# Perceiver layer on one core: the last key's share of attention moves from a matmul to a VectorE multiply-add

## The reference

```python
x = x + xattn(layernorm(x), ctx)      # softmax(q k^T / 16) v over 257 keys, one head of 256, (x + attended) @ Wo.T + bo
x = x + mixer(layernorm(x))           # in-proj to 512, 3-tap conv, silu, delta, scan over 32 steps with 16 states, out-proj
x = x + ffn(layernorm(x))             # gated, hidden 1024, inputs and weights rounded to few levels
```

## Time and profile before

| | before |
|---|---|
| median of 3 runs | 1037.6 us (1036.54 to 1038.55) |
| the profiled execution, its own time | 1038.41 us |
| its span, first to last instruction | 1036.3 us |
| busy: PE, DVE, POOL, ACT | 90%, 86%, 82%, 73% of the span |
| mean granted TensorE clock | 0.979 |

### The profile page before, as it was taken

The page is one execution under the profiler, slowest core; times in us unless marked ns, Lnnn a source line. Parts: engine busy times, 40 slices in busy tenths (PEclk is TensorE's granted clock), DMA queues, the critical chain, the costliest instruction groups (busy, mean ns, idle before and its releaser), DMA issues.

```text
span 1036.3 us, 13057 instructions
## 1 busy us (share of the span) xinstructions
PE 935.2 (90%) x4158; PEld 507.5 (49%) x4192; DVE 894.7 (86%) x1216; ACT 756.8 (73%) x1322; POOL 852.3 (82%) x616
## 2 busy tenths in 40 slices
PE   8986988999899998999899998999899998768897
PEld 6643453546345454546345554546345554434464
DVE  1636888899989999899989999899989999899964
ACT  2256658877897859877897859877897869765655
POOL 1069998899979898899979898899979898899920
PEclk9998989999999999999999999999999999988999
DMA  9814710344042610544042610544042300500000
GB/s 353 336 36 172 291 41 11 153 164 183 0 171 96 224 42 2 183 164 183 1 171 88 232 41 2 183 161 186 1 152 109 128 0 2 183 0 0 1 21 21
DMA packets 21915, 116.33 MB, mean 112 GB/s; under 512 B 3479, under 2 KB 4119, under 8 KB 9304
## 3 DMA queue, kind: packets, MB, share of 16 engines
q1 hardware_dynamic: 16232, 80.70, 21.0%
q10 hardware_dynamic: 5616, 34.81, 9.3%
HBM read 111.04 MB, written 4.46 MB: 111 GB/s over the span
## 4 chain that ended last, share of the span: by engine, by line
PE 26%; DVE 24%; ACT 19%; POOL 17%; issue 12%; DMA 1%; ACTq 0%; DVEq 0%; POOLq 0%
DVE state L1158 14%; POOL state L849 11%; PE acc L1312 11%; PE bank L1312 10%; ACT decay L920 6%; PE decay L1312 3%; POOL state L857 3%; DVE raw L1136 2%; ACT u L1019 2%; ACT u L1027 2%; ACT L920 2%; ACT soft L904 2%; DVE hm L1236 1%; POOL rstd L810 1%; DVE sg L1221 1%
## 5 line engine op out<-in xcount | busy, mean ns | idle before, releaser
L1158 DVE TENSOR_TENSOR_SCAN state<-decay,state 128x512 f32<-128x512 f32 (+1 forms) x352 | 590.7, 1696 | 35.1 <-ACT decay L920 22.8
L849 POOL TENSOR_TENSOR state<-w,brep 128x512 f32<-128x512 f32 (+1 forms) x352 | 612.0, 1766 | 0.5 <-POOL w L882 0.5
L1312 PE MATMUL acc<-state,ident 128*128 128x512 f32 x832 | 410.1, 610 | 13.7 <-DVE state L1158 12.3
L920 ACT ACTIVATE decay<-delta,neg_a 128x496 f32<-128x496 f32 x512 | 329.5, 669 | 88.1 <-DVE state L1158 86.7
L1312 PEld LDWEIGHTS acc<-state,ident 128*128 128x128 f32 x832 | 149.8, 193 | 160.5 <-issue 117.6
L857 POOL TENSOR_TENSOR state<-state 128x512 f32<-128x512 f32 x96 | 121.9, 1270 | 48.5 <-DVE state L1158 47.6
L1312 PE MATMUL bank<-out_w,u 128*128 128x256 f32 x256 | 58.2, 383 | 8.7 <-DVE u L1145 8.7
L1312 PE MATMUL bank<-xn_t,in_w 128*128 128x512 f32 x128 | 60.3, 604 | 5.0 <-DVE u L1304 3.4
L904 ACT ACTIVATE soft<-x_in,nmr,rstd 128x256 f32<-128x256 f32 x64 | 33.2, 589 | 43.0 <-POOL nmr L813 43.0
L952 ACT ACTIVATE sg<-bank,ag 128x512 f32<-128x512 f32 x64 | 43.6, 681 | 25.6 <-PE bank L1312 24.8
L1312 PEld LDWEIGHTS bank<-out_w,u 128*128 128x128 f32 x256 | 47.8, 190 | 22.8 <-DVE u L1145 15.8
(11 more groups left out here) (171 smaller groups left out, 1345.5 us busy)
## 6 DMA issues: line engine op xcount, KB each, us to landing
keys<-in_keys_t SPq DMA_DIRECT2D x32, 1028.0 KB, 5.8
brep<-b_scratch ACTq DMA_DIRECT2D x32, 1024.0 KB, 7.3
keys<-in_keys_n SPq DMA_DIRECT2D x29, 1024.0 KB
out<-x_in SPq DMA_DIRECT2D x16, 256.0 KB, 5.9
x_in<-in_x SPq DMA_DIRECT2D x14, 256.0 KB
u<-in_keys_n SPq DMA_DIRECT2D x1, 1024.0 KB
w<-in_keys_n SPq DMA_DIRECT2D x1, 1024.0 KB
delta<-in_keys_n SPq DMA_DIRECT2D x1, 1024.0 KB
```

The costliest lines, as they stand in the source:

```text
L849: nc.gpsimd.tensor_tensor(state[g % CPT][:, 0:count * tok].rearrange("p (c t) -> p c t", c=count), w[:, m, 0:tok].unsqueeze(1).to_broadcas ...
L920: last = nc.scalar.activation(decay[:, q:q + groups * GSEQ, 1:LEN], d, ACT.Exp, scale=neg_a[:, m, n + i:n + i + 1])
L1158: nc.vector.tensor_tensor_scan(flat, by, flat, 0.0, ALU.mult, ALU.add).then_inc(scan_done, 1)
L1312: return nc.tensor.matmul(o, l, r, start=first, stop=last)
```

## The change

1. `p_last`, the third transpose of `p_turn`, the `pl_t` copy of `p_evac`, and the 128x256 matmul of `attend` go, and so do `own_seq` (a 2 KB load), `pl_t` and four POOL memsets at the start.
2. The load of `keys_l` now spreads each of the four rows over 32 partitions: 128 rows, 128 KB a group. SP issues it once `z_ready` of the group two before has come, not `z_done`.
3. A new part `p_norm` on ACT multiplies the 257 weights by `rsum` before they are turned; it waits for DVE's `p_sum`.
4. `z_evac` moves from ACT to DVE: one multiply-add, z = `keys_l` x weight 256 + the PSUM sum. It waits for the matmuls of `attend` and for the keys' load.
5. All tables of "pre" and the "post" tables of phases 2 to 7 are written anew. The tables of phases 8 and 9 and the preparation are the same.

```diff
-                    if b == 0 and g < 2:
-                        sp.wait_ge(prep_p, PREP_P)
-                    else:
-                        reach(sp, z_done, *((b, g - 1) if g >= 2 else (b - 1, GROUPS - 1 + g)))
-                    sp.dma_start(keys_l[g % 2][0:GSEQ, :], t["keys_l"][FIRST_GROUP[b] + g]).then_inc(loaded, 16)
+                    if b or g >= 2:
+                        reach(sp, z_ready, *((b, g - 1) if g >= 2 else (b - 1, GROUPS - 1 + g)))
+                    sp.dma_start(keys_l[g % 2][:, :], t["keys_l"][FIRST_GROUP[b] + g].unsqueeze(1)
+                                 .to_broadcast((GSEQ, LEN, DIM))).then_inc(loaded, 16)
...
                     elif part == "exp":
                         after(act, p_turned, b, g - 1)
+                        after(act, z_ready, b, g - 1)
...
-                    elif part == "p_last":
-                        reach(act, probs_ready, b, g + 1)
-                        after(act, p_turned, b, g)
-                        nc.scalar.activation(p_last[:, :], own_seq[:, :], ACT.Copy,
-                                             scale=probs[g % 2][:, KEYS - 1:KEYS]).then_inc(p_last_ready, 1)
+                    elif part == "p_norm":
+                        reach(act, rsum_ready, b, g + 1)
+                        nc.scalar.activation(probs[g % 2][:, :], probs[g % 2][:, :], ACT.Copy, scale=rsum[:, g:g + 1])\
+                            .then_inc(p_normed, 1)
...
-                        nc.scalar.activation(to_l[0:GSEQ, :], bank[0:GSEQ, of, 2 * P:3 * P], ACT.Copy)\
-                            .then_inc(p_t_ready, 1)
-                    elif part == "z_evac":
-                        reach(act, z_done, b, g + 1)
-                        reach(act, rsum_ready, b, g + 1)
-                        after(act, z_turned, b, g if scan else g - 1)
-                        nc.scalar.activation(att_buffers(g, scan)[2][:, :], bank[:, att_banks(g, scan)[1], 0:DIM], ACT.Identity, scale=rsum[:, g:g + 1])\
-                            .then_inc(z_ready, 1)
...
+                    elif part == "z_evac":
+                        reach(dve, z_done, b, g + 1)
+                        if b == 0:
+                            dve.wait_ge(first_n_loaded[g], 32)
+                        else:
+                            reach(dve, keys_n_loaded[g % 2], b - 1, 32 * (g // 2 + 1))
+                        after(dve, z_turned, b, g if scan else g - 1)
+                        nc.vector.scalar_tensor_tensor(att_buffers(g, scan)[1][:, :], keys_l[g % 2][:, :],
+                                                       probs[g % 2][:, KEYS - 1:KEYS],
+                                                       bank[:, att_banks(g, scan)[1], 0:DIM], ALU.mult, ALU.add)\
+                            .then_inc(z_ready, 1)
...
-                        nc.tensor.transpose(bank[0:GSEQ, to, 2 * P:3 * P], p_last[:, :], ident[:, :]).then_inc(p_turned, 1)
...
-                        mm(bank[:, att_banks(g, scan)[1], 0:DIM], att_buffers(g, scan)[1][:, :], keys_l[g % 2][:, :], True, False)
```

More of the change, by code:

```diff
@@ L110 @@
[L110 to L114, removed]
+    ("z_evac", [30, 34, 63, 63]),
+    ("b_load", [78, 78, 78, 85]),
+    ("p_turn", [19, 25, 42, 42]),
+    ("s_neg", [4, 12, 25, 33]),
+    ("stats1", [0]),
+    ("x_proj", [85]),
+    ("attn_out", [65, 67]),
+    ("q_evac", [7]),
+    ("x_dbl", [76]),
+    ("evac2", [73]),
+    ("attend", [22, 33, 43, 47]),
+    ("stats2", [72]),
+    ("rstd1", [5]),
@@ new lines @@
+    ("softplus", [77, 81]),
+    ("s_bias", [4, 17, 28, 33]),
+    ("query", [1]),
+    ("add2", [40]),
+    ("dt", [87, 87, 87, 87]),
+    ("zt_evac", [23, 38, 71, 72]),
+    ("turn1", [0]),
+    ("evac1", [5]),
+    ("u_evac", [74, 74, 75, 75]),
+    ("xn2", [72]),
+    ("mix_in", [72, 73, 75, 84]),
+    ("rstd2", [21]),
+    ("exp", [7, 17, 21, 43]),
+    ("p_evac", [13, 30, 68, 70]),
+    ("add1", [7]),
+    ("p_norm", [12, 19, 42, 44]),
+    ("s_max", [1, 1, 22, 24]),
+    ("score", [4, 4, 14, 24]),
@@ L144 @@
[L144 to L157, removed]
+    ("exp", [15, 22, 28, 34]),
+    ("query", [10]),
+    ("attend", [16, 29, 30, 40]),
@@ new lines @@
+    ("p_norm", [15, 24, 31, 34]),
+    ("p_evac", [15, 28, 32, 38]),
+    ("x1", [52, 54]),
+    ("s_neg", [15, 22, 26, 32]),
+    ("q_evac", [11]),
+    ("rstd2", [51]),
+    ("s_bias", [16, 22, 26, 32]),
+    ("p_sum", [16, 23, 27, 33]),
+    ("rstd1", [0]),
+    ("add1", [45]),
+    ("stats2", [54]),
+    ("turn1", [3]),
+    ("add2", [64]),
+    ("evac1", [8]),
+    ("tap2", [61, 64, 69, 70]),
+    ("evac2", [58]),
+    ("x_proj", [73]),
+    ("softplus", [79, 87]),
+    ("z_evac", [20, 29, 32, 44]),
@@ L158 @@
+    ("silu", [69, 70, 70, 70]),
 ]
 PRE = [
-    ("x_dbl", [72]),
[L161 to L176, removed]
@@ L195 @@
[L195 to L199, removed]
+    ("xn1", [5]),
+    ("turn2", [55]),
+    ("softplus", [83, 87]),
+    ("exp", [13, 23, 29, 39]),
+    ("attn_out", [46, 46]),
+    ("score", [5, 10, 23, 28]),
+    ("xn2", [53]),
+    ("s_neg", [14, 17, 27, 34]),
+    ("rstd1", [0]),
+    ("x1", [51, 52]),
+    ("s_bias", [14, 18, 28, 38]),
+    ("mix_in", [57, 57, 59, 61]),
+    ("stats2", [52]),
@@ L200 @@
+    ("z_evac", [24, 28, 38, 43]),
+    ("tap2", [60, 61, 66, 66]),
+    ("evac1", [7]),
+    ("u_evac", [58, 60, 62, 64]),
+    ("p_norm", [17, 25, 30, 41]),
+    ("q_evac", [9]),
+    ("p_evac", [20, 25, 32, 42]),
+    ("b_load", [80, 82, 84, 84]),
+    ("p_sum", [16, 24, 29, 39]),
 ]
 PRE_END = [
-    ("x_dbl", [72]),
[L203 to L209, removed]
@@ new lines @@
+    ("zt_evac", [25, 31, 39, 45]),
+    ("z_turn", [24, 28, 39, 44]),
+    ("s_max", [13, 16, 25, 31]),
+    ("evac2", [55]),
+    ("tap0", [60, 61, 63, 65]),
+    ("x_proj", [67]),
+    ("attend", [20, 26, 32, 43]),
+    ("add2", [66]),
+    ("z_evac", [24, 28, 38, 43]),
+    ("tap2", [60, 61, 66, 66]),
+    ("evac1", [7]),
+    ("u_evac", [58, 60, 62, 64]),
+    ("p_norm", [17, 25, 30, 41]),
+    ("q_evac", [9]),
+    ("p_evac", [20, 25, 32, 42]),
+    ("b_load", [80, 82, 84, 84]),
+    ("p_sum", [16, 24, 29, 39]),
@@ L291 @@
+    ("h_scale", [22, 32, 59, 74]),
+    ("h_turn", [25, 34, 68, 76]),
+    ("h_evac", [30, 35, 71, 80]),
+    ("x_turn", [7]),
+    ("h_max", [19, 28, 54, 69]),
+    ("hidden", [15, 18, 22, 26, 42, 48, 63, 68]),
+    ("stats3", [5]),
+    ("scale_x", [12]),
 ]
```

272 lines of the change are left out of this document (109 added, 163 removed).

## The result

The changed kernel is slower: 1046.83 us median of 7 runs (1045.4 to 1052.38) against 1040.55 us of the kernel before beside it (7 runs, 1036.54 to 1043.32), a ratio of 1.0074 with a 95% interval of 1.0054 to 1.0095. The profiled execution has a span of 1045.2 us; before it was 1036.3 us. The difference of 8.9 us between these two executions (the ratio says 5.6 to 9.9 us over many) lies in two places and is reduced in two others, read from the starts of the first `w` on POOL and of each block's last `y` on DVE: +4.96 us ahead of the scan (the first `w` starts at 81.17 instead of 76.21), -0.5 in phase 1, +6.5 over phases 2 to 7, -2.1 in phase 8.

A forecast was written before the change was run, and what follows sets the result against it. The six steady phases decide, DVE and PE nearly tied: 1.56 - 0.65 - 0.71 - 0.3 = -0.1 us a phase, -0.6 in all, start and phase 1 zero, giving 1037.0 us; own range 1035.5 to 1039.7, 8-in-10 range 1029 to 1046.

The forecast's parts named there:

- rival 1: Steady phases: the gaps to be filled hang on DVE itself and move along; +0.9 us a phase, 1043 us; chance 0.32.
- Order, steady phases: Phases 2 to 7: new places fill DVE's idle gaps against 1.56 us of added work; -0.1 us a phase.
- (a): Steady phase: x_max goes from step 9 to 12, so one more scan fills DVE's 0.65 us gap; -0.65 us.
- (b): Steady phase: DVE's 0.71 us wait for PE at the second y goes; -0.71 us.
- Start: Phase 0: 0.7 us for larger keys_l loads and 0.8 for two z_evac, against PE's relief before x1; zero.
- rival 3: Start: the four-row source confines the load to 4 of 16 engines; +1.8 us, 1038.8; chance half of 0.37.
- VectorE's added work: Steady phase: four z_evac on DVE at 0.39 us each (bound 0.47), 1.56 us a phase.
- The wait for attend 3: Fourth z_evac on DVE: attend 3 ends at 715.8, DVE arrives at about 717; no wait, loss if PE over 1.2 late.
- TensorE's relief: PE's gapless stretch, 701 to 719 us: 1.1 us of work goes, only 0.71 us can reach the end.
- Rival 2: Steady phases: TensorE was the bound, its 1.1 us of relief comes out in full; -6.6 us, 1031; chance 0.31.
- (c): End of a phase: finish 2 one slot earlier spares ACT a 0.45 us wait, 0.3 counted; finish 3 gains nothing.
- (d): Steady phase: add1 on POOL moves to a time when POOL is ahead of DVE; nothing, given 11.6 us of slack.

The follow-up runs named there:

- e13: e1 with each DVE z_evac done twice from the second phase on, the first into a tile nobody reads; ratio 1.0157, phase 119.04 us.
- e4: Kernel before without the third transpose, its copy and the keys_l matmul, order unchanged; 1034.59 us, ratio 0.9971, phase 116.37 us.
- e10: e1 with x_max put back from step 12 to its old step 9; ratio 1.0056, phase 117.48 us.
- e1: Changed kernel with the last keys laid out 32 times each, so the load's source has 128 rows, not four; ratio 1.0066, phase 117.47 us.
- e6: Kernel before with z_evac as a multiply by rsum on DVE, PE's last-key work kept; 1056.64 us, ratio 1.0187, phase 118.40 us.
- e14: e1 with a 128x256 matmul of last-key rows ahead of each attend again, result overwritten, from the second phase on; 1054.01 us, ratio 1.0148, phase 118.69 us.
- e11: Kernel before with only the third finish and last h_turn at their new steps and down 2 at step 74; ratio 0.9996, phase 116.46 us.
- e8: Kernel before with the changed kernel's two feed-forward tables and nothing else; ratio 1.0150, phase 118.60 us.
- e5: e1 with z_evac as a plain copy on ACT, without the last key's share; 1056.6 us, ratio 1.0177, phase 118.23 us.
- e3: Kernel before with only the keys_l load made the 128 KB broadcast from four rows; ratio 1.0064, first w at 82.86 us.
- e2: Changed kernel with the old 4 KB keys_l load, the last key's share added for four rows only; ratio 1.0041, first w at 76.83 us.
- e9: e1 with z_evac on 32 of the 256 columns from the second phase on; ratio 1.0033, phase 117.03 us.

## Why the prediction was wrong

Forecast were 1037.0 us, no change, with the mechanism of rival 1 at 0.32 and 1043. Measured was a ratio of 1.0074, which is 1045.3 us on the 1037.6 of the forecast: above its own range, at the slow end of the wide one. Two steps failed.

- **Order, steady phases, (a) and (b): the gaps of 0.65 and 0.71 us take 1.36 of the 1.56 us.** This is the step that failed. Both gaps closed and two others of 0.88 and 0.70 us opened, one for ACT's `tanh`, one for PE's `attend`; so the idle time stayed. The phase grew by 1.01 us where -0.1 was forecast. For the wait at the fourth `z_evac` it is shown that it is a delay between two of DVE's own instructions and moves along with them: in e13 the eviction comes 1.17 us later and its wait is 0.70 us as before. e4 shows it for the second `y` (PE relieved, the wait of 0.71 us still 0.62, its chain starting from a scan). For the gap of 0.65 us there is only e10, where it changes places with the 0.88 us at no gain. It is rival 1, which had +0.9 us a phase, with the signs that the prediction gave for it: a phase over 117.4 us and over 6 us of DVE idle.
- **Start: zero, or +1.8 us by the four-row source.** Measured is +4.96 us. The mechanism of rival 3 is shown by e1 in the queue: with the same bytes from 128 rows the next issue takes 0.64 instead of 5.51 us, and the scan starts 3.34 us sooner (2.8 to 3.5 in the four profiles with a like clock). The Trainium skill ("DMA: Bandwidth & Descriptors", Rules for kernel authors) has the rule that an outermost dimension of size c below 16 confines a DMA to at most c engines. By that rule a source of four rows is slower, and e1 agrees; how many engines carried it no row here shows. The term was too small: I counted 64 KB more on four engines, 2.6 us of transfer instead of 0.7, and let 1.8 us of that reach `x1`. The queue behind the load was late by 3.6 us, and the second add of `x1` starts at 55.86 us, 3.7 later than before. The other 1.2 us lie behind that add, where the forecast had nothing, at a granted clock of 0.93 instead of 1.00. I had said that such a delay would show at the first abs sum, at 39 us; it came at 41.52, held up by a `z_evac`.
- **VectorE's added work, 0.39 us each.** Right: 0.40 us from start to start, and 0.39 in e13, where all of it came out.
- **The wait for attend 3, priced at nothing.** Wrong: 0.70 us. I let DVE reach it at about 717 and PE at 715.8, as if the two were independent. Placed by the distance from the last `y`, DVE reaches it at 716.9, as forecast, and PE is done at 717.6, 1.8 us later than forecast; 1.2 was the bound that I gave for a loss. Sums stand ahead of `attend` that wait for a scan, and the eviction starts 4.2 us behind that scan even where PE had been idle for 0.57 us (e13). Nor does PE's relief get there: in e4 `attend` 3 starts 0.4 us earlier, not 1.1. In the old order with the eviction on DVE (e6) the phase grows by 1.92 us, 0.36 more than four paces.
- **TensorE's relief: at most 0.71 us of 1.1 to show.** By itself it shows nothing (0.11, e4). In the new order it shows 1.22 (e14). The relief was also over-sized: PE's busy time fell to 108.0 us a phase, not to the 107 expected. Rival 2 therefore had a real mechanism, but it pays for part of the change instead of making it a gain: without it the phase would be 118.69.
- **(c) End of a phase, -0.3.** Measured are -0.19 us behind the second `y`, none of it in the two gaps, which sum to 2.80 us in both kernels. As predicted, `finish` 3 only changed places with a gap: 1.21 and 1.59 us became 1.58 and 1.22. That the moved `finish` 2 brought the 0.19 is not shown: e11, with `finish` 2 and the last `h_turn` at their new steps, found nothing.
- **ScalarE.** `p_norm` is 505 ns long (mean of 32), where I took 589. ACT is relieved by 1.9 us a phase, and I had 1.7. That it gives nothing by itself, as predicted, no run tests alone.
- **(d) add1, and phase 1, at nothing.** In size right: POOL is busy for 104.93 us as before, phase 1 is 0.5 us shorter. Phase 8, which I left out, is 2.1 us shorter. Its own tables are the same in all kernels, and it varies from 101.3 us (e13, granted clock 0.95) to 103.7 (e5, 0.92) in either order: e8, with new feed-forward tables alone, has 101.50 at 0.93, e3 and e4 with the old ones 103.0 at 0.90 and 0.92, e2 in the new order 103.02 at 0.90. How much is order and how much clock stays open.

The sum of measured parts is 4.96 - 0.47 + 6.49 - 2.07 = 8.9 us, the difference of the spans. e2_load4k points to both causes in times of many runs: with the transfer as it was, 1.0041 (1.0021 to 1.0060) is left of 1.0074 (1.0054 to 1.0095). The intervals just overlap.

**What stays open.** The growth of 1.01 us a phase isn't divided between DVE's work and the new order: in the old order the eviction alone costs 1.92 us (e6) and the new feed-forward places alone 2.12 (e8), and with PE's relief both together come to 1.01. Which step of a table opens the new wait for `tanh`, and whether another set of steps could take four evictions on DVE into its 6.7 us of waits, isn't settled. None of the 14 kernels beats the kernel before with the whole computation done. Adding the last key's share on POOL, which has 11 us of slack a phase, wasn't tried.

## What to carry to other kernels

An idle gap on the busiest engine is room only if what it waits for doesn't start from that engine: follow the wait back, and if it comes to one of the engine's own instructions, work put into the gap moves both ends, and each added instruction can cost its full pace (e13). It needn't come back when it is taken away: e9 gave back 0.44 of 0.81 us. Moving an operation onto the engine that everything hangs on can also put its producer in line: here some work on PE was worth 0.1 us a phase in the old order and 1.2 in the new one. And a broadcast done by the source pattern of a transfer has to be looked at for its number of rows, and for what is queued behind it on the issuing engine, not for its bytes.

## What the runs showed of the hardware

- Behind two 128 KB loads from a four-row source SP needed 5.51 us for the issue of the next transfer (5.87 in e3), behind two from a source of 128 rows 0.46 to 0.74 us (seven kernels), behind two of 4 KB 0.33: the hold shows in the row behind the transfer that causes it.
- The stretch from the second add of `x1` to the first `w` took 24.1 us at a granted clock of 1.00 (five kernels) and 25.1 to 25.6 at 0.93 (eleven). With the same instructions in phase 0, seven profiles differ by 2.7 us at the first `w`, the later ones at a lower clock from 30 to 40 us.
- A multiply-add of 128x256 with one operand in PSUM is 0.47 us long and one of 128x32 0.25. By a straight line through the two, an estimate, 0.22 us are a fixed part.
